# The first block's mask as an identity matmul: the bias is accumulated on TensorE, ScalarE moves the score bank, VectorE keeps the maxima

## What is computed

```python
lK = x @ Wlk                                   # x is layer-normed, [4096, 256]
local_scores = lQ @ lK.T * scale               # [4096, 4096]
local_scores = jnp.where(adj_matrix, local_scores, jnp.float32(-1000000000.0))
max_score = jnp.maximum(jnp.max(local_scores, axis=1, keepdims=True),
                        jnp.maximum(global_scores, es))
le = jnp.exp(local_scores - max_score)
denom = jnp.sum(le, axis=-1, keepdims=True) + ge + ee
res = le / denom @ lV + ge / denom * gV + ee / denom * eV
```

## Time and profile before

| | us |
|---|---|
| median of 3 runs | 1091.46 (1090.68 to 1092.83) |
| the profiled execution | 1091.44 |
| its span, first to last instruction | 1089.6 |
| from its start to the matmul behind score 31 (L1820) | 97.47 |
| the rest of the span | 992.1 |

### The profile page before, as it was taken

How to read it: one execution, slowest core, us unless ns; L and a number is a source line. 1 busy time by engine, 2 the same in 40 slices (tenths; PEclk the granted TensorE clock), 3 DMA queues, 4 the chain that set the end, 5 groups by cost and what they waited for, 6 DMA issues and landing times.

```text
span 1089.6 us, 15802 instructions
## 1 busy us (share of the span) xinstructions
PE 1043.4 (96%) x4996; PEld 869.2 (80%) x4996; DVE 864.3 (79%) x1534; ACT 542.7 (50%) x973; POOL 704.2 (65%) x713
## 2 busy tenths in 40 slices
PE   6878999999999999999999999998899999999998
PEld 5656887887887888788788788886787888898886
DVE  4999977798799789789879978987976775677653
ACT  4640444444445345444544444547467556655664
POOL 3774776767678677777767867768475455554451
PEclk9999999999999999999999999999899999999999
DMA  6585343453354345335335425449846547654621
GB/s 221 179 294 181 107 150 108 155 176 118 107 177 152 118 168 167 109 126 189 126 112 174 165 97 169 146 130 335 293 167 213 203 150 248 215 182 150 209 78 59
DMA packets 104341, 180.39 MB, mean 166 GB/s; under 512 B 14265, under 2 KB 45882, under 8 KB 104002
## 3 DMA queue, kind: packets, MB, share of 16 engines
q1 hardware_dynamic: 104258, 179.38, 48.8%
HBM read 143.63 MB, written 27.33 MB: 157 GB/s over the span
## 4 chain that ended last, share of the span: by engine, by line
PE 83%; DVE 5%; POOL 5%; DMA 3%; issue 2%; ACT 1%; SPq 0%; DVEq 0%; POOLq 0%; ACTq 0%
PE u_ps L1552 19%; PE s_ps L52 11%; PE s_ps L54 11%; PE s_ps L53 11%; PE u_ps L1559 9%; PE u_ps L52 3%; PE u_ps L54 3%; PE u_ps L53 3%; PE mt_ps L52 2%; PE mt_ps L54 2%; PE mt_ps L53 2%; POOL p_lo L709 2%; POOL m_lo L770 1%; PE s_ps L1607 1%; PE mb_ps L52 1%
## 5 line engine op out<-in xcount | busy, mean ns | idle before, releaser
L709 POOL TENSOR_TENSOR p_lo<-p_all,p_hi 128x512 fp32r<-128x512 f32 x224 | 295.4, 1319 | 171.8 <-PE u_ps L1559 105.2
L1285 ACT ACTIVATE p_hi<-scores 128x512 fp32r<-128x512 f32 x224 | 141.6, 632 | 360.3 <-DVE scores L866 360.0
L882 DVE TENSOR_TENSOR scores<-s_ps,bias 128x512 f32<-128x512 f32 x256 | 175.7, 686 | 84.0 <-PE s_ps L54 82.5
L1552 PE MATMUL u_ps<-p_hi,v_in 128*128 128x512 f32 x896 | 241.0, 391 | 0.0
L52 PE MATMUL s_ps<-q_hi,lnT_hi 128*128 128x512 f32 x512 | 203.0, 397 | 12.9 <-DVE scores L882 12.8
L54 PE MATMUL s_ps<-q_hi,lnT_lo 128*128 128x512 f32 x512 | 200.6, 392 | 0.0
L53 PE MATMUL s_ps<-q_lo,lnT_hi 128*128 128x512 f32 x512 | 200.4, 391 | 0.0
L1552 PEld LDWEIGHTS u_ps<-p_hi,v_in 128*128 128x128 f32 x896 | 167.2, 188 | 34.0
L701 POOL TENSOR_SCALAR bias<-adj 128x512 f32<-128x512 uint8 x256 | 164.2, 642 | 19.3 <-DVE scores L882 19.2
L866 DVE TENSOR_TENSOR scores<-scores,mb_ps 128x512 f32<-128x512 f32 x256 | 171.7, 677 | 0.8 <-PE mb_ps L1577 0.8
L903 DVE TENSOR_TENSOR kept_ps<-kept_ps,scores 128x512 f32<-128x512 f32 x232 | 162.3, 699 | 8.0
(11 more groups left out here) (212 smaller groups left out, 1777.0 us busy)
## 6 DMA issues: line engine op xcount, KB each, us to landing
v_in<-v_scratch SPq DMA_DIRECT2D x118, 512.0 KB, 3.7
adj<-in_adj SPq DMA_DIRECT2D x64, 256.0 KB, 3.9
raw<-in_wffn SPq DMA_DIRECT2D x32, 512.0 KB, 4.9
v_scratch<-vst SPq DMA_DIRECT2D x8, 1024.0 KB, 6.2
mx<-in_mx SPq DMA_DIRECT2D x18, 256.0 KB, 6.8
xg<-in_x SPq DMA_DIRECT2D x8, 512.0 KB, 4.4
uhi_scratch<-uT_high SPq DMA_DIRECT2D x8, 512.0 KB, 2.7
ulo_scratch<-uT_low SPq DMA_DIRECT2D x8, 512.0 KB, 3.6
```

What stands on the lines that cost most here:

```text
L709: nc.gpsimd.tensor_tensor(out=low_part(y), in0=whole_part(y), in1=high_part(y).bitcast(fp32), op=ALU.subtract).then_inc(plo_ready, 1)
L882: nc.vector.tensor_tensor(scores[:, t % SLOTS], s_ps[t % 3][:, :], bias[:, t % 2], ALU.add).then_inc(masked, 1)
L1285: nc.scalar.activation(high_part(y), scores[:, y % SLOTS], ACT.Exp, scale=SCALE).then_inc(phi_ready, 1)
L1552: nc.tensor.matmul(u_ps[d][:, :], values[:, x % 2, at:at + P], high_part(x), start=k == 0 and part == 0, stop=False)
```

## The change

For the steps 0 to 31 alone:

- The bias is made as `turned_bias`, the same bytes as `bias` under the type fp32r, and `MASKED` becomes -2^34, which that type holds exactly.
- `score(t)` gets a seventh matmul, with a high-part copy of the identity (`ident_high`) as weights and `turned_bias` as the moving operand, accumulated into the same bank. It waits on `bias_ready`. `bias_of(t)` on POOL waits on `score_done` of step t-2 in place of `masked`.
- `mask(t)` on DVE goes; `keep_score(t)` on ACT copies the bank to its slot and increments `masked`. DVE does only `keep(t)`.
- ACT's order in a round becomes: the copy of the last tile of the round before, the transposes, two of the four normalising instructions, the copy of tile t, the other two, the copy of t+1, `high_values`, ..., the copy of t+2. DVE does `low_turned` ahead of its keeps.
- `ident_high` lies where the third slot of the ring `v_in` comes later, so the first load of that slot on SP waits on `score_done` of step 31.

```diff
-MASKED = -1.0e9 / SCALE
+MASKED = -float(2 ** 34)
@@ SP
                 for i in range(VRING):
+                    if i == VRING - 1:
+                        sp.wait_ge(score_done, KT)
                     load_values(sp, i)
@@ POOL, bias_of
-                    wait(pool, masked, t - 1)
-                    nc.gpsimd.tensor_scalar(bias[:, t % 2], adj8[...], -MASKED, MASKED,
+                    wait(pool, score_done if t < KT else masked, t - 1)
+                    nc.gpsimd.tensor_scalar(turned_bias[:, t % 2] if t < KT else bias[:, t % 2], adj8[...], -MASKED, MASKED,
@@ DVE, the rounds
                     for i in range(4):
+                        if i == 0 and 0 < g < NG:
+                            low_turned(g, 0)
+                            low_turned(g, 1)
                         if g > 0:
-                            mask(t + i)
                             keep(t + i)
-                        if i == 0 and g < NG:
+                        if i == 0 and g == 0:
@@ ACT
+                def keep_score(t):
+                    act.wait_ge(score_done, t + 1)
...
+                    nc.scalar.activation(scores[:, t], s_ps[t % 3][:, :], ACT.Copy).then_inc(masked, 1)
@@ ACT, the rounds
                 for g in range(NG):
+                    t = 4 * g - 4
+                    if g > 1:
+                        keep_score(t - 1)
                     for k in range(KD):
                         ...
                     if g + 1 < NG:
-                        normalise(g + 1)
+                        normalise(g + 1, range(2))
+                    if g > 0:
+                        keep_score(t)
+                    if g + 1 < NG:
+                        normalise(g + 1, range(2, TG))
+                    if g > 0:
+                        keep_score(t + 1)
...
+                    if g > 0:
+                        keep_score(t + 2)
+                for t in range(KT - 5, KT):
+                    keep_score(t)
@@ PE, score
                     wait(pe, masked, t - 2)
+                    if t < KT and t % 4 == 0:
+                        pe.wait_ge(tlo_ready, t // 2 + 2)
...
+                    if t < KT:
+                        pe.wait_ge(bias_ready, t + 1)
+                        pe.wait_ge(ident_high_ready, 1)
+                        last = nc.tensor.matmul(s_ps[t % 3][:, :], ident_high[:, :], turned_bias[:, t % 2], start=False, stop=True)
+                    last.then_inc(score_done, 1)
```

More of the change, by code:

```diff
@@ L137, in gnn_moe_kernel @@
         bias = rings("bias", [P, 2, CH])
+        turned_bias = nc.alloc_sbuf_tensor_at("turned_bias", [P, 2, CH], fp32r, offset=q_at + 8 * SLOT + 4 * CH * 2)
         mxt = rings("mxt", [P, D])
@@ L213, in gnn_moe_kernel @@
         vst = before("vst", [P, 2, TG, 2 * D], fp32r)
+        ident_high = before("ident_high", [P, P], fp32r)
         def masked_parts(n):
@@ L1441, in expert, with normalise @@
                         nc.scalar.activation(y_hi[:, k], y_ps[k][:, :], ACT.Identity, bias=b2_c[:, 2 * e + k:2 * e + k + 1]).then_inc(yhi_ready, 1)
-                def normalise(g):
+                def keep_score(t):
+                    act.wait_ge(score_done, t + 1)
+                    if t == 16:
+                        act.wait_ge(wlo_ready, 4)
+                    if t == 20:
+                        act.wait_ge(w_stored, 32)
+                    nc.scalar.activation(scores[:, t], s_ps[t % 3][:, :], ACT.Copy).then_inc(masked, 1)
+                def normalise(g, tiles=range(TG)):
                     act.wait_ge(nmr_ready, g + 1)
@@ L1448, in normalise @@
                     wait(act, vlo_ready, 2 * g - 2)
-                    for j in range(TG):
+                    for j in tiles:
                         last = nc.scalar.activation(lnf[g % 2][:, j, 1:D], xg[:, g % 2, j, 1:D], ACT.Identity, scale=rstd[:, g % 2, j:j + 1],
                                                     bias=nmr[:, g % 2, j:j + 1])
-                    last.then_inc(ln_ready, 1)
+                    if TG - 1 in tiles:
+                        last.then_inc(ln_ready, 1)
                 def high_values(g):
@@ L1460, in high_weight_matrix @@
                     nc.scalar.activation(w_high[:, w], w_all[:, w], ACT.Copy).then_inc(whi_ready, 1)
+                act.wait_ge(ident_ready, 2)
+                nc.scalar.activation(ident_high[:, :], ident[:, :], ACT.Copy).then_inc(ident_high_ready, 1)
                 normalise(0)
@@ L1533, in score @@
                     wait(pe, masked, t - 2)
+                    if t < KT and t % 4 == 0:
+                        pe.wait_ge(tlo_ready, t // 2 + 2)
                     ks = slice(k * P, (k + 1) * P)
[L1535 to L1536 removed]
+                    last = split_product(nc, s_ps[t % 3][:, :], [(lnT_hi[:, d, ks], lnT_lo[:, d, ks]) for d in range(KD)],
+                                         [(q_hi[:, n % 2, d], q_lo[:, n % 2, d]) for d in range(KD)], stop=t >= KT)
+                    if t < KT:
[3 more added lines that the diff above has]
+                    last.then_inc(score_done, 1)
                 def weigh(x):
```

8 lines of the change are left out of this document (2 added, 6 removed).

## The result

The changed kernel takes 1096.76 us, median of 6 runs (1094.48 to 1099.42), beside 1091.22 us (1088.52 to 1092.83) for the kernel before on the same chip: ratio 1.0058, 95% interval 1.0043 to 1.0074. On a second chip the ratio was 1.0048 (1.0036 to 1.0060). So it is 5 to 6 us slower. The forecast was 1092.4, with a range up to 1094.9: wrong by 4.4 us.

What follows compares the result with a forecast made beforehand. A ring of waits through ACT, POOL and DVE, not VectorE, was taken to pace rounds 2 and 3. Terms -0.77 + 0.96 + 0.96 - 0.39 + 0.2 = +1.0 us on 1091.44 gave 1092.4 us, range 1090.2 to 1094.9.

Steps and rivals of the forecast that it cites:

- round 1: First round: copies start the first keep 0.64 later, two masks leave VectorE's unbroken stretch (-1.41); round 2 starts 0.77 us earlier.
- rounds 2 and 3: Two ScalarE copies of 0.48 us enter the ring, so each round grows from 8.85 to 9.81 us: +0.96 each.
- rounds 4 and 5: Load of x for group 7 is issued later, but a bias no longer waits for DVE: 19.72 against 20.11, -0.39 us.
- rounds 6 to 8: From round 6's start to the matmuls behind score 31: 21.1 us against 20.94, about even, +0.2.
- The change touches nothing in it: Beyond 109 us: one long line of TensorE matmuls, unchanged; earlier events only move its start.
- The ring: Rounds 2 and 3: ACT normalising, high values, POOL halves, biases and deviations, DVE shift, back to ACT; 8.85 us, sets the pace.
- Bounds: Nine copies on the path: 1090.2 us if half their 0.48 hid, 1093.3 if each took its full 0.58.
- VectorE as the bound: Rival, faster: VectorE paces the rounds and copies hide in ACT's idle time; -4.0, 1087.5 us; chance 0.06.
- The clock: Rival, slower: TensorE's clock falls in the last rounds, from score 23 on; +1.6, giving 1094.0 us; chance 0.25.
- The load landed later: Rival, slower: load of x lands 1 to 2 us later and passes straight through; 1093.4 to 1094.4; chance 0.09.
- the rounded type is dear for POOL: Rival: an fp32r bias takes 1.29 in place of 0.62; eight on the path add 5.4 us, 1097.8; chance 0.03.
- At nothing: Priced at zero: third values load waiting on SP for score 31, covered by ten microseconds; ACT's identity copy hidden too.

Runs made afterwards that it cites:

- after_again: The changed kernel run once more with no edit, for a second profile; ratio 1.0048 (1.0036-1.0060) to the kernel before.
- late_third_load: The kernel before plus one line of the change: the third load of values waits for score 31; ratio 0.9992 (0.9980-1.0005).
- floor_only: The kernel before with only the mask constant changed, from -1.6e10 to -2^34; ratio 1.0014 (1.0005-1.0024).
- after_old_floor: The changed kernel with the old mask constant (-1.6e10) put back; ratio 1.0038 (1.0025-1.0052) to the kernel before.
- rounded_only: The kernel before with POOL writing the first block's masks in the rounded type, old constant kept; ratio 1.0004 (0.9993-1.0014).
- two_more_copies: The kernel before with two unread 128x512 ScalarE copies added between normalising and high values in rounds 1 to 3; ratio 1.0009 (0.9996-1.0022).
- halves_shared: The changed kernel with copies behind high values, old constant, VectorE taking half the low values, POOL's deviations ahead of a mask; ratio 1.0040.

## Why the prediction was wrong

The table gives each term of the sum for after_again. "Before" is the profile that the prediction was worked out from; late_third_load, the kernel before with its one wait that costs nothing, has neither the long round 1 nor the low clock in the tail.

| term | forecast | against before | against late_third_load |
|---|---|---|---|
| round 1 | -0.77 | -1.00 | -0.40 |
| rounds 2 and 3 | +1.92 | +1.87 | +1.87 |
| rounds 4 and 5 | -0.39 | +0.06 | +0.07 |
| rounds 6 to 8 | +0.2 | +1.11 | +2.67 |
| blocks | 0 | +1.13 | +1.05 |
| rest of the program | 0 | +1.15 (other profile: +3.54) | +0.84 |

**"The change touches nothing in it", of all beyond 109 us: the step that failed.** The first hunk of the diff changes a constant that POOL uses in every block; the sections ahead of the prediction list it among what is done for the steps 0 to 31 alone and say that the change touches nothing from step 32 on, and that is wrong. I read it as a value and gave it no term, not even one at nothing. It costs 1.1 us in the blocks, 1.5 (0.5 to 2.6) in floor_only's time. "Whatever happens earlier only moves its start" was true of the matmuls' structure and false of a queue that feeds them: once in each block TensorE waits for POOL, as these rows of PE's timeline show, first in the kernel before, then in the changed one.

```profile
258.07 0.50 PE L52 MATMUL mt_ps<-m_hi,qw_hi 128*128 128x512 f32 x1 [0.76 <-POOL m_lo L770]
...
261.51 0.50 PE L52 MATMUL mt_ps<-m_hi,qw_hi 128*128 128x512 f32 x1 [0.91 <-POOL m_lo L774]
```

Between 113 and 730 us there are six such waits, 4.6 us in all before and 5.5 in the changed kernel.

**Rounds 6 to 8: mis-sized, by 0.9 us against this profile and by 2.5 against late_third_load.** I let score 25 end at 10.15 us and high values reach POOL at 11.89. They reached it 12.33 us after round 6's start, 0.4 later, and the way on from there, over two masks, two matmuls and their copies to score 28, took 0.4 to 0.5 more: matmuls behind score 31 start 22.06 us after round 6's start (100.57 - 78.51), not 21.1. With the old constant the tail is 33.71 us as well (after_old_floor); there PE stands 0.23 us for the mean on VectorE, which it does not in the changed kernel. The larger part of the miss I could not see in one profile: the 20.94 us of before hold the low clock of the earlier trace rows. In late_third_load, rounded_only and two_more_copies the clock stayed up there, as this row shows for the same stretch as the last one of the earlier trace rows, and the tail to the first weighing is 31.02 to 31.04 us and not 32.60.

```profile
93.60:96.90 3.30, 3.30 (x18) 2.78 (x17) 3.20 (x7) 0.00 (x0) 1.36 (x3) 1.00 0.57 167
```

Against these the change costs 2.7 us in the tail. Putting the last high values first gives 1.1 of it back, taking the copies out of the ring 2.0.

**Rounds 2 and 3: right, with one reading that was not.** The ring, not VectorE, set the pace, and two copies in it cost 0.92 and 0.95 a round. The estimate from the Trainium skill's "ScalarE: Activation LUTs", "What ACT_TABLE_LOAD costs", 0.52 us a copy, would have given 1.04; the trace sides with the step of 0.48. But the 2.3 us for which PE "stands in a round of this kind" come from round 4; in round 3 it was busy for 8.90 of 8.90 us already. In the changed kernel it comes out level there: the score that the mask at 53.87 waits for ends at 53.79, just when POOL's own step ahead of that mask does (52.49 + 1.30). That the matmuls did not add to the round was in part luck.

**Round 1: near, but not by the path forecast.** VectorE was to set the end of this round, shorter by two masks. In the changed kernel it stands at that place and waits for POOL's deviations. And the 11.60 us of before hold a pair of VectorE's instructions that took 2.25 us, where the pair took 0.75 in late_third_load and in the changed kernel. Rows of VectorE's timeline in before, late_third_load and the changed kernel:

```profile
36.05 2.25 DVE L1215 TENSOR_TENSOR w_all<-w_all,wlv_b 128x256 f32<-128x256 f32 x2
...
36.85 0.75 DVE L1217 TENSOR_TENSOR w_all<-w_all,wlv_b 128x256 f32<-128x256 f32 x2
...
38.45 0.16 DVE L1137 SCALAR_TENSOR_TENSOR nmr<-mv,rstd 128x4 f32<-128x4 f32 x1 [0.62 <-POOL rstd L768]
```

Against the 11.00 us of late_third_load the gain is 0.40, half of the forecast.

**Rounds 4 and 5: the load.** Its issue came 7.42 us after round 4's start (forecast 7.30), and from the moments to the next normalising it took 3.49 (3.79 worked out from the forecast). But the load took 9.23 to 9.35 us, where I kept the 8.61 of the earlier trace rows:

```profile
65.64 9.35 DMA xg<-in_x
```

In all kernels with the identity matmul it took 9.22 to 9.94 us, in those without 8.35 to 8.61, two_more_copies among them. What lengthens it no run shows.

**Bounds.** "Nine" copies is an undercount: two in each of four rounds and two or three behind are ten or eleven. That would have moved the bounds by 0.1 to 0.5 us, and not to 1096.8.

**Rivals.** VectorE as the bound fell. The clock went the other way: in the changed kernel it stays at 1.00 in the last rounds (windows above), since VectorE, without masks, comes earlier to the mean for which PE stood 1.88 us in the kernel before; the longest stand behind 92 us is 0.77 now, as this row of PE's timeline shows:

```profile
92.89 0.50 PE L1568 MATMUL s_ps<-turned_bias,ident_high 128*128 128x512 f32 x1 [0.77 <-POOL turned_bias L705]
```

A stand alone did not decide the clock in these runs: of nine profiles with the stand for the mean (1.84 to 1.95 us) the low clock followed in six; behind a stand of 2.08 us at 84.6 us in the changed kernel it did not follow (1.00 from 84 to 101 us). The load landed later, by 0.6 to 0.7. That the rounded type is dear for POOL fell; POOL's masks did get dearer, by 0.16 each, for a reason that I had not listed.

**At nothing.** The wait on SP was right.

**What stays open.** From round 1's start to the end of the blocks the changed kernel loses 3.2 to 3.4 us against before's own profile, and 5.3 to 5.6 against late_third_load or rounded_only. The medians differ by 5.5 and 5.65. So against a kernel before that is not disturbed these parts are about the whole difference. How many executions of the kernel before had the long round 1 or the low clock, the times do not tell, and the last 350 us, which vary from 349.7 to 356.3 us between profiles of all kernels, are not assigned.

## What to carry to other kernels

Ask of each hunk, a changed number too, which instructions use it in the whole program, and which engine waits for them at the narrowest place. Work moved from a full engine to an idle one is free only outside the ring that sets the pace; put it behind the step for which the others wait, and look at the last pass by itself, where nothing refills the queue. Before pricing a stretch, see in a second profile whether the first one was disturbed there, by its clock or by one long instruction, and take an engine's idle time from the very round in which it is to be used.

## What the runs showed of the hardware

- A TENSOR_SCALAR of POOL (128x512, uint8 to fp32) with constants of 2^34 and more started 0.12 us later behind the step ahead of it (1.38 against 1.26 us) than with 2^33 or 1.6e10, at the same duration of 0.62.
- A two-input subtraction of 128x512 on POOL took 1.80 us in halves_shared when a like one of VectorE (0.69) started 0.05 us before it (1.79 to 1.80 in rounds 1 to 6), and 1.29 in the kernel before. In round 7 POOL's started first, by 0.26 us: it took 1.29, and VectorE's 1.58. The Trainium skill's "SBUF — State Buffer", "Who interferes with whom", tells of one port pair that the two share under an exclusive lock. The trace agrees in kind: whichever started second took longer, POOL's by 0.51 us and VectorE's by 0.89.
